# One attention batch, reordered: the second half of the next rows is normalised later on VectorE, and two casts become maxima of equal operands

## What is computed

```
xn  = layernorm(x)
Q, K, V = xn @ Wq + bq, xn @ Wk + bk, xn @ Wv + bv        # 16 heads of 16
Qp, Kp  = relu(Q/|Q| @ proj) + 0.1, relu(K/|K| @ proj) + 0.1   # 64 features a head
KV      = sum over s of Kp[s,f] * V[s,d]
out     = (Qp @ KV) / max(Qp @ sum(Kp), 1e-6);   attn = out @ Wo + bo
probs   = softmax(xn @ router_w.T);  top 2 of 8 experts, gates normalised
rank    = position of each (token, expert) pair in the expert's list; dropped past the capacity
ffn     = gate-weighted sum of silu(xn @ w1[e]) @ w2[e] + xn
result  = x + attn + ffn
```

## Time and profile before

| | |
|---|---|
| median of 3 runs | 1320.51 us (1320.41 to 1323.15) |
| the profiled execution, its own time | 1321.38 us |
| its span | 1319.5 us |
| granted TensorE clock, mean | 0.939 of full speed |
| busy, share of the span | PE 89%, PE weight load 71%, DVE 67%, ACT 47%, POOL 55% |
| turns of the batches | b = 0 begins at 57.3 us, b = 1 at 130.8, b = 2 at 195.9, b = 3 at 260.7 |
| the experts' part | begins at 586.19 us |

### The profile page before, as it was taken

One profiled execution on the slowest core, in us unless ns is written; L12 is line 12 of the kernel. 1 busy time (PEld: TensorE's weight loads), 2 busy tenths in 40 slices (PEclk: granted clock), 3 DMA queues, 4 the chain that ended last, 5 costly groups with the idle time before them and its releaser, 6 DMA issues.

```text
span 1319.5 us, 38025 instructions
## 1 busy us (share of the span) xinstructions
PE 1173.0 (89%) x14168; PEld 943.2 (71%) x14168; DVE 882.9 (67%) x1968; ACT 621.3 (47%) x1101; POOL 723.6 (55%) x702
## 2 busy tenths in 40 slices
PE   3679798888887978459999999999999999999996
PEld 2546464656564646248888888888888888888885
DVE  6778888888887876836666666665555555555542
ACT  3476767676857675424444433433322333332221
POOL 3323465656555657753656666555555555555451
PEclk9789798979898979679999999999999999999998
DMA  4320313131322121046776667755555555555440
GB/s 110 95 34 34 82 38 78 51 66 49 68 66 34 35 34 35 2 128 156 146 149 148 146 146 153 165 98 109 98 101 99 102 101 101 106 101 103 72 74 7
DMA packets 223772, 116.03 MB, mean 88 GB/s; under 512 B 157713, under 2 KB 217234, under 8 KB 223602
## 3 DMA queue, kind: packets, MB, share of 16 engines
q1 hardware_dynamic: 190770, 78.29, 25.1%
q0 software_dynamic: 32288, 34.78, 15.8%
q10 hardware_dynamic: 544, 0.52, 0.1%
HBM read 61.82 MB, written 52.61 MB: 87 GB/s over the span
## 4 chain that ended last, share of the span: by engine, by line
PE 54%; DMA 1%; POOL 1%; issue 1%; SPq 0%; DVE 0%; POOLq 0%; ACT 0%
PE bank L994 28%; PE bank L1011 27%; POOL slot_table L1118 1%; DMA turned_rows<-xg 0%; DMA xg<-xn_split,mt 0%; DMA w_hl<-turned_rows 0%; DMA out_dram<-area,mt 0%; DMA mt<-slot_table 0%; POOL out_dram L1215 0%; SPq L472 0%; DVE area L1594 0%; POOL xg L1208 0%; POOLq L1198 0%; ACT area L676 0%; POOLq L1194 0%
## 5 line engine op out<-in xcount | busy, mean ns | idle before, releaser
L994 PE MATMUL bank<-area 128*128 128x256 f16 (+1 forms) x3408 | 376.0, 269 | 10.8 <-DVE area L1594 9.7
L1011 PE MATMUL bank<-area 128*128 x3240 | 365.4, 273 | 0.1
L994 PEld LDWEIGHTS bank<-area 128*128 x3408 | 324.4, 98 | 53.0 <-issue 12.8
L1011 PEld LDWEIGHTS bank<-area 128*128 128x128 f16 x3240 | 316.3, 98 | 37.9 <-issue 0.3
L1603 DVE TENSOR_SCALAR area<-area 128x512 f16<-128x512 f32 (+1 forms) x284 | 125.3, 441 | 281.7 <-ACT area L666 278.5
L1215 POOL DMA_INDIRECT out_dram<-area,mt x135 | 220.9, 1636 | 169.3 <-ACT area L676 135.8
L666 ACT ACTIVATE area<-bank 128x512 f32<-128x512 f32 (+1 forms) x284 | 163.6, 576 | 182.4 <-PE bank L994 180.3
L1605 DVE SCALAR_TENSOR_TENSOR area<-area 128x512 f16<-128x512 f32 (+1 forms) x284 | 189.9, 669 | 9.8
L676 ACT ACTIVATE area<-bank,mt 128x256 f32<-128x256 f32 x135 | 57.1, 471 | 288.9 <-PE bank L1011 288.9
L1118 POOL DMA_INDIRECT slot_table<-area x128 | 137.3, 1072 | 98.4 <-PE bank L866 41.3
L1208 POOL DMA_INDIRECT xg<-xn_split,mt x135 | 141.8, 1050 | 44.6 <-issue 39.8
(11 more groups left out here) (194 smaller groups left out, 1408.6 us busy)
## 6 DMA issues: line engine op xcount, KB each, us to landing
turned_rows<-xg SPq DMA_DIRECT2D x256, 64.0 KB
w_hl<-turned_rows SPq DMA_DIRECT2D x64, 256.0 KB, 3.1
area<-in_x_dram SPq DMA_DIRECT2D x16, 512.0 KB, 5.3
xn_split<-area SPq DMA_DIRECT2D x128, 64.0 KB, 2.2
w_raw<-in_w_dram SPq DMA_DIRECT2D x64, 128.0 KB, 3.9
out_dram<-area SPq DMA_DIRECT2D x30, 256.0 KB, 3.6
area<-in_w_dram SPq DMA_DIRECT2D x14, 512.0 KB, 5.5
xg<-xn_split,mt POOLq DMA_INDIRECT x135, 3.3
```

Source lines behind the costliest of these rows:

```text
L994: mm = nc.tensor.matmul(big[j][:, i2 * n:(i2 + 1) * n], we[:, bass.ds(e * EXPERT + (k * 2048 + wl * 1024 + c * P), P)], moe_xT[t % XT][:, ...
L1011: mm = nc.tensor.matmul(yb[:, a * D:(a + 1) * D], hT[u % 2][:, c, hl, a * P:(a + 1) * P], we[:, bass.ds(e * EXPERT + off, D)], start=(c == ...
```

## The change

It has four places. VectorE normalises half 1 of the next batch after `place_read`, and no longer ahead of the copy of the sums. ScalarE writes the high part of half 1 after `xT_copy` of half 0, and no longer ahead of the copy of `cn`. TensorE transposes half 1 after both groups of the second half's query features, and no longer between the groups. The copy of the reciprocals and the cast of `kvf` are written as `tensor_tensor` with the same operand twice and the maximum, which gives the same values.

```diff
@@ act_turn
             q_relu(act, b, 0, 4, PAIRS)
-            if body:
-                xn_high(act, b + 1, 1)
             nc.scalar.copy(cn_b..., take(act, phase, "attn", "cn", b)...).then_inc(attn_taken, 1)
             if body:
                 xT_copy(act, phase, b + 1, 0)
+                xn_high(act, b + 1, 1)
             resid_rows(act, b, 0)
@@ pe_turn
             attend(pe, phase, b, HT - 1)
+            q_features(pe, b, 1, 1)
             if body:
                 x_transpose(pe, phase, b + 1, 1)
-            q_features(pe, b, 1, 1)
@@ v_over_norm
-            ch.step(v.tensor_copy(dst[:, :, :, HD:HD + 1], rnf))
+            ch.step(v.tensor_tensor(dst[:, :, :, HD:HD + 1], rnf, rnf, ALU.max))
@@ kv_build
-            v.tensor_copy(kv_hl[:, 0], kvf).then_inc(kvf_ready, 1)
+            v.tensor_tensor(kv_hl[:, 0], kvf, kvf, ALU.max).then_inc(kvf_ready, 1)
@@ dve_turn
                 normalise_rows(dve, b + 1, 0)
-                normalise_rows(dve, b + 1, 1)
             dve.wait_ge(kv_tile_done, (b + 1) * NT)
...
             place_read(dve, phase, b)
+            if body:
+                normalise_rows(dve, b + 1, 1)
             if not body:
```

## The result

The changed kernel takes 1329.46 us (median of 4 runs, 1328.12 to 1333.07) against 1320.67 us for the kernel before: a ratio of 1.0065, 95% interval 1.0051 to 1.0079, or 6.7 to 10.4 us slower. The side was forecast, the size was not: 3.1 us were forecast, and 1329.46 lies above the range, which ended at 1328.0.

What follows compares the result with a forecast made beforehand. TensorE's own work was taken to bound the experts' part, and chains of waits between engines the turns. Relu delays summed to 3.1 us, 1324.5 us for the profiled execution; median forecast 1323.6 us, range 1316.5 to 1328.

Steps and rivals of the forecast that it cites:

- What bounds the kernel: Experts' part is TensorE's own work, unedited; turns are set by wait chains, ending at the second half's first relu.
- The earlier copy of the sums: VectorE, turn start: copy starts 1.29 us earlier; after the wait for the first relu, 0.97 us are left.
- The maximum: VectorE's split of `kvf`: waits for GpSimd's `x_low` like the cast, 0.14 us dearer; in turn 2 the 0.97 is lost.
- The rival of the escape: Two equal inputs escape GpSimd's blocking and the kernel gets faster: 1313.5 us; chance 0.15.
- The moved normalising: VectorE after the counts: 1.35 us within the old idle 1.59, drain no later; ScalarE's relu 0.9 us late in turn 2.
- the second rival: GpSimd's constant part blocks the moved normalising: 0.4 us more a turn, 5.5 to 6 in all, 1326 us; chance 0.15.
- The slack of turns 0 and 6: ScalarE's 2.17 us wait for tile ab3 in turn 6 covers its loss, leaving 0.14 us; turn 0 alike.
- The sum: Relu delays over turns 0 to 7: 0.1 - 0.4 + 0.9 + 0.5 + 0.9 + 0.9 + 0.1 + 0.1 = 3.1 us.
- the clock: Left out of the sum: TensorE's granted clock may shift as waits move, 0.3 us a turn either way, 2 in all.
- TensorE's transposes, "zero": Half 1's transposes, 1.07 us, fit into TensorE's 2.04 us idle ahead of tile ab4: zero, at most 1.07 a turn.
- The range: From 1316.5 us (the copies alone escaping) to 1328 us (blocked normalising with the clock's 2 us against).

Runs made afterwards that it cites:

- the moves alone: The changed kernel with the two maxima written as copy and cast again, all three moves kept: 1.0057 (1.0041 to 1.0074) against the kernel before.

## Why the prediction was right in direction and wrong in size

**What bounds the kernel: right.** The experts' part kept its length to 0.4 us, and the loss sits in the turns, at the relu that was named.

**The earlier copy of the sums: right, its gain too large.** It starts 3.94 us after the start of turns 1 to 4, 1.30 earlier (1.29 forecast), and in turn 2 the first `q_low` then waits for its relu (0.80 us). Of the 1.30 us 0.4 were left there, not the forecast 0.97, since the relus themselves came 0.5 us later against the turn's start.

**The maximum: right.** Blocked while `x_low` runs and 0.14 us dearer when free. The maxima by themselves cost 0.4 us (-0.9 to 1.7), forecast 1.1. The rival of the escape is out.

**The moved normalising "lies within its old idle 1.59", 1.35 us long: this step failed.** It takes 1.96 us, because GpSimd's constant part blocks it, so the first drain starts 0.9 us later against the turn's start and not "no later than before", and ScalarE's wait for the half, forecast 0.3, was 1.08. This was the second rival, held at 0.15 and priced at 0.4 us a turn. Measured it is 0.58 in every turn, and I had argued it away from the pace of the instruction (256 columns 0.33 us apart), which turned out to say nothing about the blocking. The Trainium skill (VectorE: DVE Perf Modes, section "The perf-mode tier table"), which lists fp32 `tensor_scalar` in SBUF among the operations of the mode with both ports, was nearer: the trace agrees with the blocking that would follow from it, 1.37 against 1.96 us. The pace does not agree: that table of the Trainium skill gives 1227 ns for 2048 fp32 elements, by which 256 would take 0.15 us (an estimate from the page's figure), and here they come 0.33 us apart.

**The slack of turns 0 and 6: there, but used up.** The forecast left a loss of 0.1 us in each; against the end of `x_low` it was 0.6 and 0.5. In turn 6 before, ScalarE waited 2.17 us for tile ab3; in the changed kernel no such wait is left, since ab3 was ready first in all seven turns. The slack covered the forecast delay and not the further 0.58. Against the turn's start the relu came 0.2 and 1.6 us later; the rest of turn 6's 1.6 is `x_low`'s own lateness, 1.0.

**The sum.** Turn by turn, from the end of `x_low` to the relu, the seven turns lose 0.6, 0.1, 1.5, 1.1, 1.5, 1.4 and 0.5, together 6.7. The forecast was 3.0, and seven times 0.58 is 4.1 more, which makes 7.1; turn by turn it makes 0.7, 0.2, 1.5, 1.1, 1.5, 1.5 and 0.7. With the price of the normalising put right the rest of the working fits each turn to 0.2 us. Beside it stand 1.7 us by which `x_low` itself comes later against the turn's start, as the turn's first relus do. I can't ascribe them: in the profiled executions of like kernels on chips of the same speed, the starts of these first relus, summed over the seven turns, differ by 3 us (38.2 to 41.3; 39.9 in the kernel before and 41.7 in the changed one), and in the moves alone `x_low` came 0.4 us earlier in sum. The eight relus take 2.2 us more, with TensorE's lower clock, and the rest of the turns 1.2 less; the forecast had allowed 2 us for the clock either way. 6.7 + 1.7 + 2.2 - 1.2 = 9.4, as measured in this execution.

**TensorE's transposes, "zero": right in the total** (0.9985 for them alone), wrong as to why. They are not simply covered: they had kept TensorE at work in a gap, and in this kernel's trace the clock is lower behind the gap and higher later.

**The range** ended 1.5 us too low, because the blocked normalising was priced at 0.4 us a turn: with the clock's 2 us that reaches 1328. With its measured 0.58, 4.1 us in all, the sum is 1327.7, and 1329.7 with the clock's 2 us.

## What to carry to other kernels

Before an instruction of VectorE is moved, look at what GpSimd does at the new place, not only at whether VectorE is idle there: here GpSimd's two-input work in SBUF held VectorE's casts (1.02 us against 0.30), its two-input operations (2.10 against 0.44) and a `tensor_scalar` with scalars from SBUF (four in 1.96 against 1.37). A cast gained nothing by being written with two equal inputs; keeping the two engines apart by one wait gave 9 us where the rewriting gave none, but the same wait cost 2.8 us (1.5 to 4.1) in the order of before, so it has to be measured with the order it is meant for. And a piece of work moved behind idle time on one engine moves its readers too: the free place on VectorE was ahead of it on ScalarE's path.

## What was not expected of the hardware

This is the normalising by its line in the changed kernel (count, ns min/median/max):

```profile
L1296 DVE TENSOR_SCALAR area<-area x64: 396/406/734, 12.0 to 483.2; 128x256 f32<-128x256 f32 x64
```

- A `tensor_scalar` of 256 float32 columns with two scalars from SBUF takes 0.41 us alone and is held by GpSimd's two-input work: four of them took 1.37 us with GpSimd idle, 1.96 with the end of its constant part beside them, and 2.44 with nearly all of it.
- A gap of 2.10 us on TensorE, otherwise filled with 1.07 us of transposes, went with a granted clock at its lower level (1.2 GHz) over part of the features behind it in every turn, where it had been in four of seven; the same sixteen transposes then took 1.89 us. With VectorE's normalising put back, the features behind a gap of 2.4 to 2.6 us ran at the higher level in three turns of seven. The seven turns together were no longer for it (465.9 us in both traces).
